# Identities multiplied ahead of the attention, a last row tile in two transfers, weights prepared in two parts, and four steps moved in TensorE's order

## What is computed

```python
h = relu(layernorm(x)); x = x + attention(h, adj)        # 4 heads of 32, softmax over the neighbours
h = relu(layernorm(x)); x = x + h @ W_self + (adj @ h / deg) @ W_neigh
h = relu(layernorm(x)); x = x + gru(relu((adj @ h) @ W_msg.T + b_msg), h)
h = relu(layernorm(x)); x = x + hyperbolic_layer(h, adj)  # embed, adj @ tangent vectors, bottom product
```

## Time and profile before

| | us |
|---|---|
| median of three runs | 593.09 |
| the profiled execution's own time | 593.54 |
| its span, first to last instruction | 591.7 |
| PE busy in the span | 556.8 (94%) |
| DVE busy | 346.8 (59%) |
| ACT busy | 217.2 (37%) |
| POOL busy | 99.1 (17%) |
| mean granted clock of TensorE | 0.984 of full |

### The profile page before, as it was taken

How to read it: one execution, slowest core, us unless ns; L and a number is a source line. 1 busy time by engine, 2 the same in 40 slices (tenths; PEclk the granted TensorE clock), 3 DMA queues, 4 the chain that set the end, 5 groups by cost and what they waited for, 6 DMA issues and landing times.

```text
span 591.7 us, 12155 instructions
## 1 busy us (share of the span) xinstructions
PE 556.8 (94%) x4562; PEld 350.6 (59%) x4562; DVE 346.8 (59%) x1504; ACT 217.2 (37%) x588; POOL 99.1 (17%) x102
## 2 busy tenths in 40 slices
PE   4679899999999999999999999999999999999990
PEld 4579899999994544444444545555554444555540
DVE  5894822343224463333315588898888863676787
ACT  4530011100110200000032587888789665532433
POOL 3880000000000010000000121212222210330322
PEclk9979999999999999999999999999999999999996
DMA  8999999999950000000000001001100020111011
GB/s 235 108 108 108 109 109 108 108 109 108 109 55 4 1 19 1 1 0 1 14 5 19 13 24 37 16 29 30 36 1 20 18 90 1 37 54 37 18 37 36
DMA packets 23897, 29.17 MB, mean 49 GB/s; under 512 B 11296, under 2 KB 11936, under 8 KB 23840
## 3 DMA queue, kind: packets, MB, share of 16 engines
q0 software_dynamic: 8704, 16.78, 28.2%
q1 hardware_dynamic: 15136, 11.62, 6.5%
HBM read 72.43 MB, written 4.19 MB: 129 GB/s over the span
## 4 chain that ended last, share of the span: by engine, by line
PE 79%; DVE 15%; issue 2%; POOL 2%; ACT 1%; DMA 1%; SPq 0%; DVEq 0%; POOLq 0%
PE acc L1605 46%; PE acc L1413 10%; PE acc L1414 10%; PE acc L1443 4%; PE acc L1450 3%; PE acc L1501 2%; PE acc L1433 1%; POOL rs L1068 1%; DMA x<-x_rows 1%; PE acc L1537 1%; POOL region_st L1068 1%; DVE x L1048 1%; DVE region_op L999 1%; DVE x L1051 1%; DVE hs_a L384 1%
## 5 line engine op out<-in xcount | busy, mean ns | idle before, releaser
L1605 PE MATMUL acc<-adj,hs_a 128*128 128x512 fp8e4 x1024 | 227.8, 379 | 0.9 <-issue 0.9
L1605 PEld LDWEIGHTS acc<-adj,hs_a 128*128 128x128 f16 x1024 | 99.3, 98 | 114.0 <-issue 1.4
L1413 PE MATMUL acc<-region_op,adj 128*128 128x133 f16 x1024 | 127.6, 224 | 5.2 <-issue 3.6
L1414 PE MATMUL acc<-region_op,adj 128*128 128x132 f16 x1024 | 127.7, 223 | 0.0
L1605 PE MATMUL acc<-adj,region_op 128*128 128x512 fp8e4 x512 | 118.3, 379 | 0.0
L1413 PEld LDWEIGHTS acc<-region_op,adj 128*128 128x128 fp8e4 x1024 | 101.1, 99 | 7.0 <-issue 3.7
L1414 PEld LDWEIGHTS acc<-region_op,adj 128*128 128x128 fp8e4 x1024 | 101.0, 99 | 0.0
L1605 PEld LDWEIGHTS acc<-adj,region_op 128*128 128x128 f16 x512 | 49.3, 98 | 54.4
L1068 POOL TENSOR_TENSOR region_st<-region_st,small 128x4 f32<-128x4 f32 (+1 forms) x39 | 44.9, 1151 | 200.7 <-ACT w L1202 128.9
L1068 POOL TENSOR_TENSOR rs<-rs,small 128x4 f32 (+3 forms) x27 | 30.9, 1145 | 273.5 <-DVE rs L401 270.8
L1181 ACT ACTIVATE hs_a<-rowbuf 128x512 f32 (+1 forms) x8 | 5.0, 630 | 115.9 <-DVE rowbuf L407 115.9
(11 more groups left out here) (251 smaller groups left out, 689.4 us busy)
## 6 DMA issues: line engine op xcount, KB each, us to landing
adj<-adj_pieces POOLq DMA_DIRECT2D x32, 512.0 KB, 65.9
p_rows<-rowbuf SPq DMA_DIRECT2D x8, 256.0 KB, 2.1
region_op<-p_rows SPq DMA_DIRECT2D x8, 256.0 KB, 3.1
out_rows<-x SPq DMA_DIRECT2D x7, 256.0 KB, 2.1
x<-x_rows SPq DMA_DIRECT2D x3, 512.0 KB, 7.3
region_st<-matrices SPq DMA_DIRECT2D x1, 768.0 KB, 9.5
x<-x_rows SPq DMA_DIRECT2D x2, 256.0 KB, 4.2
hT<-region_op SPq DMA_TRANSPOSE x32, 2.4
```

The lines of the kernel that those rows point to most:

```text
L1413: mm(dst[:, 0:HI], adj8[:, it, jt, :], op0[:, jt, 0:HI], start=(jt == 0), stop=False)
L1414: last = mm(dst[:, 0:LO], adj8[:, it, jt, :], op0[:, jt, HI:OPW], start=False, stop=(jt == NT - 1))
L1605: last = mm(dst, hs[:, jt, part, :], adj8[:, c * TG:(c + 1) * TG, jt, :], start=(k == 0), stop=(k == 2 * NT - 1))
```

## The change

TensorE multiplies a float32 identity by itself, 14 times in front of the wait for `ext_ready` and 26 times in front of the wait for `wlo_ready` (which precedes the first attention matmul). The results go to a bank that nobody reads. The last row tile of the adjacency matrix is fetched by two transfers of half its size, and TensorE waits for the second after half of that tile's matmuls. `prepare_weights` ends after the nine square matrices; the rest, `prepare_gates`, follows VectorE's second group. Four more matmuls of block 1 stand before the flag is read, with the three steps of `both_zero` shifted; in layer 3, four matmuls of SECOND stand in front of `update_back`, and four more of THIRD in front of the last `own_part`.

```diff
@@ constants
+KEEP_1, KEEP_2 = 14, 26
@@ VectorE, prepare_weights
                 me.link(v.reciprocal(w_scale, floors))
-                me.link(v.reciprocal(msg_scale, msg_unscale))
-                me.step(v.tensor_tensor(msg_bias, b_msg, msg_scale, ALU.mult))
-                me.link(v.tensor_tensor(msg_scale, msg_scale, floor[:, M_MSG:M_MSG + 1], ALU.mult))
                 for m in range(NM):
                     me.step(v.tensor_scalar(raw[:, m, :], raw[:, m, :], w_scale[:, m:m + 1], None, ALU.mult))
...
-                me.step(copy(w_unscale, floors))
+                me.link(copy(w_unscale, floors))
+                v.memset(small[:, 51:52], 0.0).then_inc(S["w16_ready"], 1)
+
+            def prepare_gates(me):
+
+                me.link(v.reciprocal(msg_scale, msg_unscale))
+                me.step(v.tensor_tensor(msg_bias, b_msg, msg_scale, ALU.mult))
+                me.link(v.tensor_tensor(msg_scale, msg_scale, w_unscale[:, M_MSG:M_MSG + 1], ALU.mult))
                 me.step(v.tensor_scalar(ih_scale, w_scale[:, M_HR:M_HN + 1], msg_unscale, SPLIT, ALU.mult, ALU.mult))
...
-                v.memset(small[:, 51:52], 0.0).then_inc(S["w16_ready"], 1)
...
             prepare_weights(me)
             attend(1, None)
+            prepare_gates(me)
@@ GpSimd, fetch
-                pool.dma_start(dst, src).then_inc(adj_in[it], 16)
+                if it < NT - 1:
+                    pool.dma_start(dst, src).then_inc(adj_in[it], 16)
+                else:
+                    pool.dma_start(dst[:, 0:1, :], src[:, 0:1, :]).then_inc(adj_in[it], 16)
+                    pool.dma_start(dst[:, 1:2, :], src[:, 1:2, :]).then_inc(S["adj_last"], 16)
@@ TensorE
+            def keep_busy(count):
+
+                for _ in range(count):
+                    mm(bank[6][:, 0:D], ident[:], ident[:], start=True, stop=True)
+
+            keep_busy(KEEP_1)
             pe.wait_ge(S["ext_ready"], 1)
...
+            keep_busy(KEEP_2)
             pe.wait_ge(S["wlo_ready"], 1)
...
-            AHEAD_1 = 44
-            both_zero = {45: own_transposes, 50: own_self, 57: neighbours}
+            AHEAD_1 = 48
+            both_zero = {49: own_transposes, 54: own_self, 60: neighbours}
...
-                attend(it, range(NT)).then_inc(S["acc_full"], 1)
+                if it < NT - 1:
+                    attend(it, range(NT)).then_inc(S["acc_full"], 1)
+                else:
+                    attend(it, range(PIECE_T))
+                    pe.wait_ge(S["adj_last"], 16)
+                    attend(it, range(PIECE_T, NT)).then_inc(S["acc_full"], 1)
...
             embed(FIRST - 2)
+            aggregate(SECOND, 8, 12)
             update_back(FIRST - 1)
-            aggregate(SECOND, 8, 40)
+            aggregate(SECOND, 12, 40)
...
-            aggregate(THIRD, 20, 26)
+            aggregate(THIRD, 20, 30)
             own_part(FIRST - 1)
             embed(FIRST - 1)
...
-            aggregate(THIRD, 26, 48)
+            aggregate(THIRD, 30, 48)
```

More of the change, by code:

```diff
@@ L241, in build_graph_stack @@
             "consts_set", "dve_step",
-            "ve_ready", "rs_ready", "wa_full", "xn0_ready", "tr0_full", "hT0_ready", "xp_full", "xp_read",
+            "ve_ready", "rs_ready", "wa_full", "adj_last", "xn0_ready", "tr0_full", "hT0_ready", "xp_full", "xp_read",
             "sq0_ready", "var0_ready", "rs0_ready", "pwa_ready", "ext_ready", "gen_step", "extT_full", "diag_ready", "extall_ready", "spread_ready", "spreadall_ready", "shift_ready", "w_ready", "whi_ready", "wlo_ready", "y_ready", "hi0_ready", "op0_ready",
@@ L718, in general_attention @@
                 dve.wait_ge(turn, TURN_END + 1)
-                prepare_weights(Steps(dve, S["gen_step"]))
+                steps = Steps(dve, S["gen_step"])
+                prepare_weights(steps)
+                prepare_gates(steps)
                 with dve.Fori(0, OWN_EARLY) as g:
```

## The result

| | before | changed |
|---|---|---|
| median (lowest to highest), nine runs each | 593.41 us (592.66 to 594.93) | 595.32 us (594.51 to 596.77) |
| the profiled execution's own time | 593.54 us | 594.51 us |
| its span | 591.7 us | 592.7 us |
| mean granted clock | 0.984 | 0.989 |

The ratio is 1.0033, with a 95% interval of 1.0021 to 1.0046: the change makes the kernel slower by 0.33%, or 1.9 us. I had forecast 591.1 us and faster.

What follows compares the result with a forecast made beforehand. TensorE, busy 94% of the span, was taken as the bound. Terms +0.7 - 1.77 + 0 - 0.86 - 0.1 = -2.0 us took the median from 593.09 to 591.1 us; range 589.3 to 592.6.

Steps and rivals of the forecast that it cites:

- Four matmuls ahead of the flag: At the flag, four more matmuls fit beside the read and branch while TensorE would stand still: -0.86 us.
- the shifted steps: The three `both_zero` steps at the flag keep their distance to the branch: 0 us.
- Rival (b): The flag's read waits for TensorE's matmuls, or code is placed less luckily: -1.1 us, or 592.0 us; chance 13%.
- my slow rival: Before the attention the clock falls anyway and the second identity block runs at half pace: +3.5, 596.6 us; chance 7%.
- then -0.6: At the flag, if the read starts only after the four matmuls are issued, their 0.24 us of issue leaves -0.6.
- The identities: Before the attention, two records each hold the full clock but overshoot the operand by 1.8 us: +0.7 us net.
- Weights in two parts: In front of tile 8, TensorE no longer waits for VectorE's division: -1.77 us (-1.6 to -1.8).
- The last tile in two transfers: At tile 31 the transfers have already landed: 0.0 us; it would matter if TensorE came over 2 us earlier.
- Layer 3: The wait at `update_back` goes, but a new 0.7 us wait behind L928 takes the gain back: -0.1 us.

Runs made afterwards that it cites:

- the pair of kernels with 44 and 48: The first experiment's kernel with 44 instead of 48 matmuls of block 1 ahead of the flag, 592.25 us, beside the first experiment itself (48), 592.53 us.
- the fastest kernel: Changed kernel with 9 and 15 identities in place of 14 and 26, nothing put in the never executed path: 590.75 us, ratio 0.9959.
- the first experiment: Changed kernel with 32 more float16 matmuls (64 instructions) in the general path that is never executed: 592.53 us, ratio 0.9983.

## Why the prediction was wrong

**The step that failed is "Four matmuls ahead of the flag: -0.86 us".** It was +1.27 in the profiled execution. I took TensorE to run at full pace once it goes on behind the branch, priced the shifted steps at 0 and gave the added instructions no term at all. What the runs showed: TensorE lands 12 instructions ahead of a boundary, and what lies behind the boundary comes 2.9 to 3.3 us after the landing. Six matmuls cover 1.3 us of that; the start behind the stop is 3.08 us after the landing, where at full pace it would be 6 x 0.216 = 1.30: 1.78 us lost. Rival (b) had the words "code is placed less luckily", but gave it the price of an unhidden read, 592.0 us. I had no bound for it on the slow side, and my slow rival was another mechanism, the clock, which did not occur.

The Trainium skill ("Runtime: NRT & Kernel Launch", section "Instruction fetch mechanics") says that instructions are refilled in 16 KiB blocks of 256, that crossing a boundary is mostly hidden, and that a taken branch out of the window forces a fetch. The traces agree with the 256 as far as the stops go (28 instructions behind the landing where 12 - 240 + 256 is 28), and one of the two queues of instruction packets on the page of the changed kernel (number, MB, share) has packets of 16.4 KB; the other, q14, has 20 of 8 KB, and which engine a queue serves is not shown:

```profile
q8 instruction: 39, 0.64, 0.4%
```

The two queues have 59 packets together. TensorE alone has 9284 matmuls and weight loads on that page, which would take 73 blocks of 128 and 37 of 256; so, if a packet is one block, 128 is out.

The traces do not agree that the boundary is hidden in the first 3 us behind a taken branch. I had drawn on this section for the restart and stopped there.

**The term had a second error.** Without the stop, -0.86 would have been about -0.6: -0.37 by the pair of kernels with 44 and 48, -0.52 by the changed kernel and the one before, and -0.58 by the means of all kernels. I had kept "then -0.6" for the case in which the read begins only after the issue of the queued matmuls, with 0.24 us as the most that four of them cost. The mean of 0.28 fits that case; the scatter of 0.4 us between kernels with the same number is too wide for more. Whether it is their issue was not measured by itself.

**The identities: right mechanism, size off.** Forecast +0.7, measured +1.35. Two records each, no fall of the clock, the slow stretch gone: all as forecast, and the gain of the clock, 1.95, was measured as 33.34 - 31.39 = 1.95. The cost was 3.30 in place of 2.65: the first block delays the transposes by 0.90 (29.14 - 25.01 against 27.96 - 24.73; forecast 0.8), the gap between the blocks is 30.57 - 29.14 = 1.43 (forecast 1.2), and 52 records take 5.91, or 0.1137 each (forecast 5.6, at 0.108). I had scaled the projection's 0.111 down by 128/132; the records show no gain from fewer columns. The attention's start at 36.48 also holds 0.28 us of a later input, a scatter between executions: the same 28 records start anywhere between 24.60 and 26.02 in the kernels that have them.

**Weights in two parts: right.** -1.79 for -1.77, with the wait gone as worked out. Undone alone it costs 1.92 us in the trace, and 1.45 to 2.3 by the medians and the ratios.

**The last tile in two transfers: right,** 0.0. It would have been 0.36 with the transfers as the bound, "if TensorE came over 2 us earlier": in the fastest kernel it does.

**Layer 3: right.** The wait in front of `update_back` is gone, the one in front of `own_part` is 0.43, the new one 0.54, the sum -0.15 for -0.1.

**The sum.** With the measured terms in place of the forecast ones, the change without the second stop is +1.35 - 1.79 - 0.52 - 0.15 = -1.1 us, or -0.96 with the -0.37 of the other pair; the first experiment measured 592.53 - 593.49 = -0.96 (by its interval 0.4 to 1.5 less). The second stop adds 1.78, and -0.52 + 1.78 is the +1.27 of the ledger within 0.01: the change comes to +0.7. The medians of the changed kernel and of the first experiment differ by 2.8 us, the interval by the ratios is about 2 to 4. The traces put 1.57 of it on the stop and the restart; that leaves 1.2 us, of which the profiled pair has 0.78 in the start, where the two kernels are the same. Whether this is scatter stays open.

## What to carry to other kernels

When instructions are added ahead of a taken branch, in whatever path, the place where the branch lands moves against the blocks in which code comes; look behind each such landing for a stop that ends in "issue", and move the landing by code that is never executed to see what it costs. Filling an idle stretch to hold the clock pays only as far as the fill ends before the work that it stands in front of; measure the filler's own pace, and give it fewer pieces than fit. Look at the granted clock behind a stop as well: the one of 2.39 us was followed by 3 us at half clock. A wait that was removed pays in full only until the next bound: here the transfers of the adjacency matrix in the fastest version, and the last operand group in layer 3.

## What the runs showed of the hardware

- Behind the taken branch the first instruction past the next boundary starts 2.91 to 3.33 us after the landing, in six kernels: 2.99 with 4 instructions between them, 3.08, 3.33, 3.07 and 2.91 with 12, and 3.07 with 28. By the two stops at 12 and 28, 240 instructions of padding apart, and by the packets on the page, the boundaries are 256 instructions apart. With 76 or more instructions between them no stop was seen; between 28 and 76 nothing was measured.
- Float32 matmuls of 128 columns have two records each, 0.111 us apart in a block of 28 and 0.114 in one of 52, at a granted clock of 1.00. The Trainium skill ("TensorE: Matmul & The Clock Gate", section "Back-to-back issue gap") has about 81 ns for a stream of weight load and matmul pairs with 128 columns; these did not reach it.
- The granted clock was 0.50 from 194 to 197 us, behind a stop of TensorE of 2.39 us in which it had stayed at 1.00; behind stops of 1.61 and 1.86 us it stayed at 1.00.
- More matmuls queued ahead of the read of the flag made TensorE's restart later on average: 5.39 to 5.76 us after the first of 20 (three kernels), 5.68 to 6.06 after the first of 24 (eleven).
